# A fixed pause for GpSimd in place of a wait, ahead of each pair's gathers in a graph-attention kernel

## What is computed

```python
q, k, v = x @ Wq + bq, x @ Wk + bk, x @ Wv + bv      # 8 heads of 16
e = edge_attr @ We
k_e, v_e = k[src] + e, v[src] + e
alpha = einsum('ehd,ehd->eh', q[dst], k_e) / sqrt(16)
a = exp(alpha - segment_max(alpha, dst)[dst])
out = segment_sum(a / segment_sum(a, dst)[dst] * v_e, dst)
x_r = x @ Wskip + bskip
beta = sigmoid([out, x_r, out - x_r] @ Wbeta)
out = layernorm(beta * x_r + (1 - beta) * out) * gamma + beta_ln
return layernorm(x + x + relu(out))
```

## Time and profile before

| What | Value |
|---|---|
| Median of three runs | 2459.15 us (2456.94 to 2463.15) |
| Profiled execution | 2454.78 us |
| Span of its profile | 2453.0 us |
| Time outside the span | 1.8 us |
| Mean granted TensorE clock | 0.824 of full speed |
| Head of pair 3 to head of pair 195 | 114.76 to 2372.94 us: 192 pairs of 11.76 us |
| Busy: PE, DVE, POOL, ACT | 72%, 70%, 61%, 33% |

### The profile page before, as it was taken

The page is one execution under the profiler, slowest core; times in us unless marked ns, Lnnn a source line. Parts: engine busy times, 40 slices in busy tenths (PEclk is TensorE's granted clock), DMA queues, the critical chain, the costliest instruction groups (busy, mean ns, idle before and its releaser), DMA issues. The chain is left out here.

```text
span 2453.0 us, 35080 instructions
## 1 busy us (share of the span) xinstructions
PE 1762.1 (72%) x10434; PEld 1597.7 (65%) x10434; DVE 1720.9 (70%) x2897; ACT 805.9 (33%) x1889; POOL 1492.3 (61%) x1580
## 2 busy tenths in 40 slices
PE   7667777777777777777777776777767776767773
PEld 5566766766666666666667665676667666667662
DVE  6566665666666666677677777777777777777886
ACT  0122222222322332333333333333343334334446
POOL 0466666666666666666666666666666666666650
PEclk9788888888887888888887889879887888887885
DMA  8755656656555555555655555555566566656641
GB/s 302 243 186 185 198 179 201 193 181 199 184 166 171 167 185 169 171 182 163 186 176 167 188 173 178 179 174 186 171 198 191 183 196 191 194 178 200 198 144 48
DMA packets 231807, 449.01 MB, mean 183 GB/s; under 512 B 42082, under 2 KB 151752, under 8 KB 218974
## 3 DMA queue, kind: packets, MB, share of 16 engines
q1 hardware_dynamic: 156304, 241.36, 30.1%
q0 software_dynamic: 75312, 205.36, 27.9%
HBM read 404.57 MB, written 41.99 MB: 182 GB/s over the span
## 5 line engine op out<-in xcount | busy, mean ns | idle before, releaser
L784 POOL DMA_INDIRECT kv<-kv_tab,src_all x1498 | 1421.8, 949 | 706.7 <-issue 409.7
L1020 PE MATMUL sum_ps<-wv,hot_en 128*128 128x136 f32 x3136 | 563.7, 309 | 367.5 <-issue 345.7
L1020 PEld LDWEIGHTS sum_ps<-wv,hot_en 128*128 128x128 f32 x3136 | 464.7, 209 | 420.2 <-issue 413.3
L908 PE MATMUL q_all<-q_win,hot_ne 128*128 128x128 f32 x3136 | 452.5, 306 | 3.2 <-DVE prod L1505 1.9
L908 PEld LDWEIGHTS q_all<-q_win,hot_ne 128*128 128x128 f32 x3136 | 443.6, 225 | 7.0 <-issue 6.2
L1505 DVE TENSOR_TENSOR prod<-q_all,kve 128x1024 f32<-128x1024 f32 x196 | 240.0, 1225 | 288.4 <-remote 273.6
L1494 DVE TENSOR_TENSOR kve<-kv,e_ps 128x768 f32<-128x768 f32 (+1 forms) x392 | 407.4, 1080 | 7.1 <-issue 5.3
L1168 ACT ACTIVATE wt_ps<-logit,used_b 128x64 f32<-128x64 f32 x196 | 62.2, 318 | 1061.1 <-issue 862.5
L893 PE MATMUL e_ps<-we,tab_buf 128*128 128x128 f32 x1568 | 307.2, 361 | 112.2 <-issue 88.1
L893 PEld LDWEIGHTS e_ps<-we,tab_buf 128*128 128x128 f32 x1568 | 282.7, 268 | 141.4 <-issue 134.0
L893 PE MATMUL e_ps<-we,ea 128*128 128x128 f32 x1568 | 318.6, 377 | 72.9 <-issue 51.8
(11 more groups left out here) (151 smaller groups left out, 1096.1 us busy)
## 6 DMA issues: line engine op xcount, KB each, us to landing
ea<-eaT SPq DMA_DIRECT2D x49, 1024.0 KB
row_b<-rel_row SPq DMA_DIRECT2D x98, 512.0 KB
tab_buf<-eaT SPq DMA_DIRECT2D x49, 1024.0 KB
kv<-kv_tab,src_all POOLq DMA_INDIRECT x1498
q_win<-q_tab SPq DMA_DIRECT2D x252, 64.0 KB
sum_tab<-sums SPq DMA_DIRECT2D x251, 59.5 KB
kv_tab<-tab_buf SPq DMA_DIRECT2D x33, 384.0 KB, 3.9
logit<-sum_tab SPq DMA_DIRECT2D x49, 136.0 KB
```

The source lines that it names most:

```text
L784: pool.indirect_dma_start(out=head_rows(q) if u == t == 0 else kv[:, s, t, :], out_offset=None, in_=kv_tab[:, :], in_offset=bass.IndirectO ...
L908: mm = pe.matmul(q_ps[u][:, t * P:(t + 1) * P], hot_ne[:, 2 * par + u, t * P:(t + 1) * P], q_win[:, 2 * par + min(u, parts(q) - 1), :], st ...
L1020: mm = pe.matmul(sum_ps[1 if wide else u][:, 0:AC], hot_en[:, 2 * par + u, t, :], wv[:, 2 * par + u, t, :], start=(t == 0 and not (wide an ...
```

## The change

Pair 2 and each later one no longer wait for `q_ok` of pair `q - 2` at their head. In its place GpSimd clears a scratch row of 700 floats in one partition, and each such clearing first waits for the one before it. The wait for the head buffer (`kve_head(q - 3)`) and those of the second and fifth gathers stay. Nothing else reads the row.

```diff
+REST = 700
...
+        rest = sb("rest", [1, REST])
...
+        rest_ok = sem("rest_ok")
...
                         if q >= 2 and u == 0 and t == 0:
-                            pool.wait_ge(q_ok, 2 * (q - 2) + 2)
+                            if q > 2:
+                                pool.wait_ge(rest_ok, q - 2)
+                            pool.memset(rest[:, :], 0.0).then_inc(rest_ok, 1)
                             if q >= 3:
                                 pool.wait_ge(kve_ok, kve_head(q - 3))
```

## The result

| | before | after |
|---|---|---|
| median of 4 runs each | 2458.34 us (2456.94 to 2463.15) | 2761.55 us (2756.88 to 2774.05) |
| ratio | | 1.124, 95% interval 1.122 to 1.126 |
| span of the profile | 2453.0 us | 2760.2 us |
| mean granted TensorE clock | 0.824 | 0.757 |
| mean distance of `products`, pair 3 to 195 | 11.76 us | 13.33 us |

The change makes the kernel 303 us slower. The direction and the mechanism were forecast; the size was 95 us short and lies 21 us outside the range. In the changed kernel lines have moved by five: the gathers are L789, the clearing L781, `kve` L1494 and L1499, `prod` L1510, `q_all` L913, the edge one-hot (`hot_en`) L1557.

What follows compares the result with a forecast made beforehand. Not a full engine but PE's completions, held 1.41 us per gather, bound the kernel at 11.76 us a pair. 2454.8 + 208 (192 pairs, 1.08 us more each) + 4 for the median gave 2667 us; range 2395 to 2741.

Steps and rivals of the forecast that it cites:

- The hold and what ends it: On PE's completions: each gather mostly holds them 1.41 us, 11.58 us from head gather to release, until POOL pauses.
- The clearing: On POOL before a pair's head gather: clearing 700 floats adds 0.98 us, with bounds 0.68 to 1.33.
- the lower bound: The clearing's cost on POOL if it overlaps with its neighbours' gaps: 0.68 us.
- the 1.3 us that a release needs: Least pause of POOL between a pair's eighth gather and the next head for PE's completions to be released.
- Where POOL stops: At a pair's second gather, awaiting `kve`, in 4 of 5 pairs: 11.58 us, then POOL goes on 1.65 us later.
- the bare hold: Length of a pair whose `kve` is ready in time: eight gathers at 1.41 us, 11.3 us.
- 0.8 x 13.23 and 0.2 x 11.3: Stopping and unstopped pairs, weighted: mean pair 12.84 us, 1.08 more than 11.76, +208 us over 192 pairs.
- The rival A: POOL's pause suffices or PE keeps up: pair between 11.3 and 11.58 us, 2405 us in all, faster; chance 0.33.
- The rival B: At the head, the clearing starts only when the hold ends: pair 12.28 us, +100 us, 2559 us; chance 0.13.
- The rival C: The second gather's `kve` wait ends where the head's wait ended: pair 11.76 us, 2459 us, no change; chance 0.12.
- The range: Whole kernel's time, 2395 to 2741 us; the top has all pairs stopping at 13.23 us.
- The rule of the Trainium skill: Work on the engine with the highest occupancy; POOL, at 61%, is not it, so the change's sum would be zero.

Runs made afterwards that it cites:

- e10: Kernel before with the `q_ok` wait dropped and nothing cleared, on a chip with the hold: 2868.5 us against 2484.63, ratio 1.155.
- e12: Changed kernel with 1,800 floats cleared instead of 700, on a chip with the hold: 2668.57 us against 2484.63 for the kernel before, ratio 1.075.
- e1: Kernel before with the `q_ok` wait dropped and nothing cleared, on a chip without the hold: 2113.83 us against 2112.5, ratio 1.001.
- e5: Changed kernel itself, unedited, on a second chip without the hold: 2213.27 us against 2113.05 for the kernel before, ratio 1.047.

## Why the prediction was right or wrong

**The hold and what ends it: right.** The step that carried the argument was that each gather holds most of PE's completions for 1.41 us and a long enough pause of POOL lets them go. The records of the semaphores bear it out: the burst comes after 10.14, 11.49, 13.01, 22.71 and 34.09 us for 7, 8, 9, 16 and 24 gathers, 1.40 to 1.41 us for each one more from 8 to 16 and 24. The word "mostly" is needed. In the kernel before, all 192 updates of the query spread fall into the burst, but of the 170 recorded for the edge part, 145 come within the run of gathers. e10 (wait gone, no clearing: slower by 15.5%) and e11 (clearing there, wait kept: no change) separate the wait's part from the clearing's. A small slip beside it: PE's clock isn't 0.7 to 0.9 in every slice, the last has 0.5; nothing hangs on that.

**The clearing: 0.98 us taken, 0.53 measured.** The duration from the earlier trace rows was right: 0.68 us worked out, 0.672 measured. What was wrong is the lower bound: I had not allowed that the clearing hides part of the next gather's 0.30 us. Under the hold it made no difference to the forecast, since either value is short of the 1.3 us that a release needs. That figure was near: 0.53 doesn't release, 1.45 (e12) releases in about half the pairs.

**Where POOL stops: right in place, wrong in size, and this is the step that failed.** It does stop at the second gather, for `kve`, in all 106 stops. But "POOL goes on 1.65 us later", taken from the earlier trace rows, is the row of a pair that has a release to itself, and POOL doesn't even stop in it: it was idle for its usual 0.30 us. I had "4 of 5 pairs" stop, each with its own hold of 8 gathers. I also had one pair in five at the bare hold, 11.3 us, as if it ended by itself. In fact `kve` of the first pair is there in time, so that POOL runs on over 16 gathers and stops once in two pairs: 106 stops in 192 pairs, 87 of them after 16 gathers. Behind such a stop most of what PE finished in 22 us is seen at once, and DVE stands one step further back in its order, at `hot_en` in 72 of the 87. It takes 4.56 us until POOL goes on. The 18 stops after 8 gathers behave as forecast: 11.25 and 1.55, together 12.81 us, where I had 13.23. So the terms 0.8 x 13.23 and 0.2 x 11.3 were in fact 174 pairs of 13.41 and 18 of 12.81.

The sum with the measured terms: two pairs took 2 x 11.76 = 23.52 us before and take 22.26 + 4.56 = 26.82 now, 3.30 more, 1.65 a pair. The mean over all pairs, from head to head, is 13.35 - 11.76 = 1.59 us more, and 192 times that is 305 us: all of the measured 303. My 12.84 us was 0.51 short, 98 us.

**The rival A, faster, failed.** The pause was 0.53 us. Even at 1.45 us in e12, above the 1.3 from which A was to decide, half the pairs still stop and the ratio is 1.075.

**The rival B, the clearing queues behind the hold, failed.** It starts 0.00 us after the gather's end, and in e11, inside the hold, it costs nothing.

**The rival C, the same wait elsewhere, failed.** A pair isn't 11.76 us but 13.35.

**The range.** It took all pairs at 13.23 us as its worst case. A hold that spans two pairs was not among the cases, though the first 24 gathers had shown that holds can be long. And none of the cases had the hold missing, by which the change costs 4.7%.

**The rule of the Trainium skill** ("Perfetto Trace Analysis", Identifying the Most-Contended Engine) that the fullest engine is the one to work on would have given no change. It misled in both conditions: under the hold the number of gathers since the last release sets the pace; and without it, e1's pace is POOL's at 71% busy, beside DVE at 82%. POOL's 0.30 us before each gather is not counted as busy, but it isn't free either.

**What stays open.** What the hold is: the traces show when PE's completions are seen, not what delays them. Slower transfers of the gathers it is not: the packets of their queue took 33.0% of e1's span of 2108.2 us and 24.3% of e10's 2866.1, 696 us on each of 16 engines both times. Why it is there on some runs and not on others: two chips showed none and a third showed it, as did the first comparison, each for all runs of its set, so it may be the chip or something else that lasted as long (the other programs of the set are one candidate, P in e5's expectation). That the first comparison had it is luck for the forecast, which never asked. Why e10 takes 6.22 us behind a release and the changed kernel 4.56: in e10 DVE restarts more often at `prod` (43 of 79), earlier in its order, which fits but wasn't tested.

## What to carry to other kernels

A wait that an engine seems to lose time in can be what lets another engine's results through. Before it is dropped, ask what else that engine's stream of instructions holds up, and price the next stop by a row in which as much is queued as will be there then, not by a row of the calm case. And a saving or a loss that hangs on such an interplay should be tried on more than one chip: here the same edit costs 4.7% or 12.4%, and the bare removal of the wait 0 or 15.5%.

## What the runs showed of the hardware that wasn't expected

- The same kernel took 2112.5, 2113.05 and 2484.63 us on three chips, with spreads within each of 0.5% or less. Its gathers hardly differ (0.95 us each, 1.251 us apart in e1 and 1.254 in e10); only the completions of PE are seen late, and the mean granted clock of the kernel without clearing and wait falls from 0.925 (e1) to 0.759 (e10).
- Where PE's completions are held, most of them are held for 1.42 to 1.45 us for each 128-row gather since the last release, over runs of 7, 8, 9, 16 and 24 gathers, while POOL's own records show gathers 1.254 us apart. The query spread's semaphore changes a median of 6.28 us after PE's record of it ends (before), and 0.01 us where nothing is held (e1).
- A row of one partition is cleared in 0.672, 1.338, 1.588 and 1.838 us for 700, 1,500, 1,800 and 2,100 floats: 0.83 ns a float. Behind a clearing the next gather starts after 0.16 us, where it is 0.30 behind another gather.
